# A Mamba-2 block and a quantized feed-forward block on one core: the state's product as two column tiles of 64 rows

## The chip, the cores and the metric

One core of a Trainium2 chip. The metric is the device time of one execution in microseconds (us). The engines are TensorE (PE, with its weight loads as PEld), VectorE (DVE), ScalarE (ACT), GpSimd (POOL) and SyncE (SP, which issues the transfers).

## What is computed

Two residual blocks over x of 4 x 1024 x 256 in float32: x plus the layer norm of a Mamba-2 layer, then x plus the layer norm of a feed-forward layer with 4-bit weights. The part that the change touches is the Mamba-2 layer's recurrence, cut here to its products:

```python
Y_diag = jnp.einsum('bclgn,bcsgn,bgrcls,bcsgrp->bclgrp', Cc, Bc, Lmat, xdt)
decay_states = jnp.exp(A_cs[..., -1:] - A_cs)
states = jnp.einsum('bcsgn,bgrcs,bcsgrp->bcgrpn', Bc, decay_states, xdt)
...
def step(S, inp):
    d, st = inp
    S_new = S * d[..., None, None] + st
    return (S_new, S)
...
Y_off = jnp.einsum('bclgn,bcgrpn,bgrcl->bclgrp', Cc, prev_states, state_decay)
Y = (Y_diag + Y_off).reshape(B_, nc, CHUNK, NHEADS, HEADDIM)
```

There are 8 heads of 64 channels (512 together) and 128 state rows. The kernel works in chunks of 128 positions. `states`, for one chunk, is a product of 128 state rows x 128 positions with 128 positions x 512 channels: this is "the state's product".

## The kernel before

The 4096 positions are cut into blocks of 512, each of two halves of 256, each of two chunks of 128. A loop runs 7 times over iterations (i = 2 to 8) after a first stretch of its own (`FIRST`) and before a last one (`LAST`). In one iteration the Mamba-2 part of one block is interleaved with the feed-forward part of the block before. Every engine works through a list of steps written out by hand (`ORDER`, L70; `FIRST`, L103), where `st:1` is step `st` for chunk 1 of the block, "<" marks the block before and ">" the next one. Engines synchronize by semaphores, one for each kind of step; `count` gives the value to wait for.

TensorE's steps that matter here:
- `gu:n` (L1219) and `dn:n` (L1228): the feed-forward's gate and up products (two times six matmuls with 512 columns, into the banks `fb`) and its down product (12 matmuls with 256 columns, into `db`). All go through the helper `split_matmul`, whose matmul is L1073; the operands are split in two float32r parts.
- `yo` (L1169): the state before the chunk times C, one float32 product of 128 x 128 weights and 512 columns.
- `yd` (L1177): the diagonal product. For each of 8 heads two matmuls, one for each 64 rows of the output (`l0`), with 64 columns of `lmat` as weights and 64 columns of `xdt` moving (L1184). The rows `l0` to `l0 + 63` of the bank are also the columns of TensorE's array that the matmul uses.
- `st` (L1188): the state's product, one float32 product with all 128 columns of the transposed B (`gb[:, 2 + c, :]`) as weights and the 512 columns of `xdd` moving (L1193), into one bank. It waits for GpSimd's `xdd` (L548), ScalarE's copy of B (L673) and for the reader of the product that had the bank before (`bank_read`: three banks `mb` are used in turn by all Mamba-2 steps). VectorE adds the result to the state (`state_`, L927).
- `xt`, `xtr`, `yt`, `x1t`: transposes (L1092, L1166, L1199, L1216); `ip`, `z`, `out`: projections (L1073 into `mb`).

A float32 matmul stands in the trace as two weight loads and two matmuls, a float32r one as one of each.

In the loop's order on TensorE, the four state products stand so:

```python
dn:3< yd:0 st:0 gu:6< yt:0 xtr:1 dn:4< out:0 yo:1 dn:5< yd:1 st:1 xt:1 gu:7< yt:1 ...
gu:12< dn:10< yo:2 xtr:2 xt:0> gu:13< yd:2 st:2 dn:11< yt:2 dn:12< xtr:3 out:2 yo:3 yd:3 gu:14< st:3
dn:13< yt:3 gu:15< ...
```

So `st:0`, `st:1` and `st:2` stand directly behind a diagonal product, and `st:3` between `gu:14` and `dn:13`. In `FIRST` three of six are apart from `yd` (`st:2`, and `st:1` and `st:3` of the next block). 32 state products run in all.

Of the kernel before, what the change touches and what calls it, by code (L numbers as in the profile page):

```python
# [31 lines left out]
HEADS, HD, DI, NSTATE, TAPS = 8, 64, 512, 128, 4  # L32
# [194 lines left out]
def build(nc, u, in_proj, conv_w, conv_b, dt_bias_in, a_log, d_skip, norm_w, out_proj,  # L227
          packed, scales, out):
    ctx = ExitStack()
    with ctx:  # L230
        def sb(name, shape, dt=F32, stack=ctx):
            return stack.enter_context(nc.sbuf_tensor(name, shape, dt))

        def sem(name):
            return ctx.enter_context(nc.semaphore(name))
# [81 lines left out]
        gb = sb("gb", [P, 4, CH])  # L317
        xdd = sb("xdd", [P, DI])
# [45 lines left out]
        s = {name: sem("s_" + name) for name in per_block}  # L364
        whole = ("gate", "up", "gelu", "inter", "hi", "lo", "down", "var4", "rstd4", "d_read", "fin_link")

        def count(name, i, k):

            absent = 0 if name in whole else per_block[name] // 2
            return i * per_block[name] - absent + (k + 1)  # L370
# [12 lines left out]
        m_bank = {use[:2]: mb[n % 3] for n, use in enumerate(m_uses)}  # L383
# [670 lines left out]
        def _(pe):  # L1054
            def bank_read(uses, use, i):

                u = [v[:2] for v in uses].index(use)
                it = i - AWAY[uses[u][2]]
                v, back = u, 0
                while not isinstance(it, int) or it - back >= -1:  # L1060
                    v -= 3
                    if v < 0:
                        v, back = max(w for w in range(len(uses)) if w % 3 == u % 3), back + 1
                    name, k, whose, step = uses[v]
                    if there(step, k, it - back + AWAY[whose]):
                        pe.wait_ge(s[read_by[name]], count(read_by[name], it - back + AWAY[whose], k))
                        return
# [120 lines left out]
            def st(i, par, q):  # L1188
                c = q % 2
                pe.wait_ge(s["xdd"], count("xdd", i, q))  # L1190
                pe.wait_ge(s["gbs"], count("gbs", i, q // 2))
                bank_read(m_uses, ("st", q), i)
                pe.matmul(m_bank["st", q][:], gb[:, 2 + c, :], xdd[:], start=True, stop=True).then_inc(s["st"], 1)  # L1193

            def yt_(i, par, q):
                pe.wait_ge(s["y"], count("y", i, q))
# [31 lines left out]
            def dn(f, par, n):  # L1228
# [5 lines left out]
                for t in tiles(f):  # L1234
# [5 lines left out]
                last.then_inc(s["down"], 1)  # L1240

            drive(pe, "pe", dict(xt=xt, ip=ip, cs=cs, ct=ct, seg=seg, z=z, gb=gb_, xtr=xtr, yo=yo, yd=yd, st=st, yt=yt_, out=out_,
                           x1t=x1t_, gu=gu, dn=dn), identity)

# [40 lines left out]
```

## Time and profile before

| | us |
|---|---|
| median of 3 runs | 996.51 (996.26 to 999.14) |
| the profiled execution | 1000.16 |
| its span, first to last instruction | 998.4 |
| TensorE matmuls busy | 909.1 (91%) |
| VectorE busy | 789.2 (79%) |
| ScalarE busy | 599.2 (60%) |
| GpSimd busy | 338.6 (34%) |

The first 60 us or so load and unpack weights. From then on TensorE is nearly always busy, in iterations of about 112 us each. Matmuls overlap in the pipeline: a record's duration holds its way through the array, and a group of records that follow each other takes less than their sum. The chain of waits counts each instruction from where the one before it ended, and is the better view for what a step costs in sequence. The granted clock of TensorE is 1.00 (2.4 GHz) in the steady iterations, and 0.5 in some stretches of the first 90 us.

### The profile page before, as it was taken

What the parts mean: (1) busy time and instruction counts of PE and PEld (TensorE: products, weight loads), DVE (VectorE), ACT (ScalarE), POOL (GpSimd) and SP (SyncE); (2) the same over time, 40 slices, a digit from 0 to 9 for tenths busy, and PEclk for the clock granted to TensorE, in tenths of its full rate; (3) what the DMA queues carried; (4) which work ended last, traced back from release to release, by engine and by line L of the source; (5) the groups of instructions that cost most, each with busy time, mean ns of one, the idle gap of its engine ahead of it and who ended that gap; (6) DMA issues with size and microseconds to landing.
All of it is one profiled execution on the core that took longest, in us unless ns stands there. A gap on an engine that the chain in (4) does not pass through costs nothing.

```text
span 998.4 us, 17980 instructions
## 1 busy us (share of the span) xinstructions
PE 909.1 (91%) x6560; PEld 786.0 (79%) x6560; DVE 789.2 (79%) x2079; ACT 599.2 (60%) x1013; POOL 338.6 (34%) x346
## 2 busy tenths in 40 slices
PE   1556797999999999999999999999999999999987
PEld 0445695888888788888888798878888798888887
DVE  6898777898879988898879988898879888886132
ACT  5955847574737665674737565674838565672222
POOL 2022233334252424334152424234152524234332
PEclk9767799999999999999999999999999999999999
DMA  7300000000001000000001000000000000000000
GB/s 225 124 1 11 1 12 1 12 11 2 11 2 32 1 12 1 11 23 1 12 1 33 1 11 1 11 23 1 12 1 33 2 11 2 5 18 1 1 22 11
DMA packets 14087, 17.70 MB, mean 18 GB/s; under 512 B 1712, under 2 KB 10416, under 8 KB 14000
## 3 DMA queue, kind: packets, MB, share of 16 engines
q1 hardware_dynamic: 13136, 16.53, 5.4%
q8 instruction: 52, 0.85, 0.4%
q14 instruction: 35, 0.29, 0.1%
q10 hardware_dynamic: 864, 0.03, 0.0%
HBM read 12.36 MB, written 4.19 MB: 17 GB/s over the span
## 4 chain that ended last, share of the span: by engine, by line
PE 58%; DVE 22%; ACT 7%; issue 6%; POOL 5%; DMA 1%; SPq 1%; DVEq 0%; POOLq 0%; ACTq 0%
PE fb L1073 23%; PE mb L1073 14%; PE db L1073 11%; DVE xc L882 7%; PE mb L1193 2%; DVE lmat L856 2%; DVE hid L990 2%; DVE lmat L901 2%; POOL yg L557 2%; DMA wd_raw<-in_packed 1%; PE mb L1174 1%; PE mb L1199 1%; PE mb L1184 1%; POOL hl L569 1%; ACT xc L651 1%
## 5 line engine op out<-in xcount | busy, mean ns | idle before, releaser
L569 POOL TENSOR_TENSOR hl<-hid,hl 128x512 fp32r<-128x512 f32 (+1 forms) x144 | 169.5, 1178 | 407.9 <-ACT hl L705 407.7
L1073 PE MATMUL fb<-x1t,wg 128*128 128x512 f32 (+1 forms) x864 | 215.9, 386 | 5.3 <-DVE x1t L984 5.3
L1073 PE MATMUL db<-wd,hl 128*128 128x256 f32 x1536 | 216.6, 289 | 2.2 <-POOL hl L569 2.0
L1073 PEld LDWEIGHTS db<-wd,hl 128*128 128x128 f32 x1536 | 197.4, 189 | 17.8 <-issue 10.1
L1073 PE MATMUL fb<-x1t,wu 128*128 128x512 f32 (+1 forms) x864 | 206.1, 375 | 3.3 <-ACT hid L698 3.3
L1073 PEld LDWEIGHTS fb<-x1t,wu 128*128 128x128 f32 x864 | 153.6, 192 | 36.7 <-ACT hid L698 4.8
L1073 PEld LDWEIGHTS fb<-x1t,wg 128*128 128x128 f32 x864 | 146.3, 193 | 30.9 <-DVE x1t L984 6.7
L990 DVE TENSOR_TENSOR hid<-fb,hid 128x512 f32<-128x512 f32 (+1 forms) x144 | 90.2, 627 | 78.1 <-PE fb L1073 67.6
L705 ACT ACTIVATE hl<-hid 128x512 fp32r<-128x512 f32 (+1 forms) x144 | 83.6, 581 | 106.1 <-DVE hid L990 77.8
L882 DVE SCALAR_TENSOR_TENSOR xc<-raw,cw,xc 128x256 f32<-128x256 f32 x288 | 132.9, 529 | 9.6 <-ACT xc L651 8.3
L698 ACT ACTIVATE hid<-fb 128x512 f32<-128x512 f32 (+1 forms) x144 | 78.1, 548 | 84.8 <-PE fb L1073 81.1
L1073 PE MATMUL mb<-xnt,wi 128*128 128x256 f32 x576 | 80.0, 292 | 17.9 <-DVE xnt L794 15.6
L539 POOL TENSOR_TENSOR rs<-ve,neg_half 128x1 f32<-128x1 f32 (+2 forms) x89 | 58.8, 661 | 100.2 <-DVE ve L780 30.9
L1073 PEld LDWEIGHTS mb<-xnt,wi 128*128 128x128 f32 x576 | 74.2, 197 | 19.5 <-issue 18.8
L548 POOL TENSOR_TENSOR xdd<-xdt,ex 128x512 f32<-128x512 f32 x32 | 33.4, 1043 | 116.4 <-DVE xdt L910 116.4
L698 ACT ACT_TABLE_LOAD x51 | 65.4, 1283 | 0.9
L856 DVE TENSOR_SCALAR lmat<-mb,ct_ 128x128 f32<-128x128 f32 x208 | 56.5, 342 | 2.2 <-PE mb L1130 2.2
L1073 PE MATMUL mb<-wi,xnt 128*128 128x264 f32 (+1 forms) x384 | 55.1, 295 | 3.4 <-ACT xc L651 3.4
L1073 PE MATMUL mb<-wo,yt 128*128 128x256 f32 x384 | 54.6, 293 | 3.5 <-issue 2.1
L1073 PEld LDWEIGHTS mb<-wi,xnt 128*128 128x128 f32 x384 | 51.2, 200 | 3.5 <-issue 3.5
L1073 PEld LDWEIGHTS mb<-wo,yt 128*128 128x128 f32 x384 | 49.5, 197 | 4.8 <-issue 2.9
L557 POOL TENSOR_TENSOR yg<-yg,t 128x512 f32<-128x512 f32 x32 | 42.1, 1317 | 20.4 <-DVE t L917 20.4
(150 smaller groups left out, 1360.4 us busy)
## 6 DMA issues: line engine op xcount, KB each, us to landing
xin<-in_u SPq DMA_DIRECT2D x16, 256.0 KB, 2.7
out<-xb SPq DMA_DIRECT2D x16, 256.0 KB, 2.2
wg_raw<-in_packed SPq DMA_DIRECT2D x4, 256.0 KB, 13.2
wg_raw<-in_scales SPq DMA_DIRECT2D x4, 256.0 KB
wu_raw<-in_packed SPq DMA_DIRECT2D x4, 256.0 KB, 13.6
wu_raw<-in_scales SPq DMA_DIRECT2D x4, 256.0 KB
wd_raw<-in_packed SPq DMA_DIRECT2D x4, 256.0 KB, 13.2
wd_raw<-in_scales SPq DMA_DIRECT2D x4, 256.0 KB
```

The lines of the kernel that those rows point to most:

```text
L539: pool.tensor_tensor(dst, src, neg_half[:, 0:src.shape[1]], ALU.pow).then_inc(s["rstd" + name], 1)
L548: pool.tensor_tensor(per_head(xdd[:]), per_head(xdt[:]), spread_heads(ex[:, q // 2, 1, q % 2, :]), ALU.mult).then_inc(s["xdd"], 1)
L557: pool.tensor_tensor(yg[:], yg[:], t1[:], ALU.add).then_inc(s["yskip"], 1)
L569: pool.tensor_tensor(hl[:, hs, n % 2, 1, :], hid[:, hs, n % 2, :], hl[:, hs, n % 2, 0, :].bitcast(F32), ALU.subtract).then_inc(s["lo"], 1)
L698: act.activation(hid[:, halves(f), n % 2, :], by_half(f_bank["gate", n], f), ACT.Gelu_apprx_tanh).then_inc(s["gelu"], 1)
L705: act.activation(hl[:, halves(f), n % 2, 0, :], hid[:, halves(f), n % 2, :], ACT.Copy).then_inc(s["hi"], 1)
L856: last = dve.tensor_scalar(lmat[:, c, h0 + h, :], m_bank["seg", k][:, CH * h:CH * h + CH], ct_[:, 0, r:r + 1], 0.0, ALU.subtract, ALU.min)
L882: ins = dve.scalar_tensor_tensor(out=xc[:, ct, :], in0=raw[:, slot, e, tap:tap + SUB], scalar=cw[:, ct, tap:tap + 1], in1=xc[:, ct, :], op ...
L901: dve.tensor_tensor(lmat[:, c, :, :], lmat[:, c, :, :], gb[:, c, :].unsqueeze(1).broadcast_to([P, HEADS, CH]), ALU.mult).then_inc(s["m"], 1)
L990: dve.tensor_tensor(hid[:, halves(f), n % 2, :], by_half(f_bank["up", n], f), hid[:, halves(f), n % 2, :], ALU.mult).then_inc(s["inter"], 1)
L1073: last = pe.matmul(ps, lhs(a, k), rhs(b, k), start=start and n == 0, stop=stop and n == len(todo) - 1, skip_group_check=check)
L1193: pe.matmul(m_bank["st", q][:], gb[:, 2 + c, :], xdd[:], start=True, stop=True).then_inc(s["st"], 1)
```

## The change

The state's product is done as two matmuls, each with 64 of the 128 state rows: the weights are 64 columns of the transposed B, the output is half of the bank's rows, and both have all 512 columns of `xdd` moving. The array is then addressed in halves of 64 columns, as in `yd`. The semaphore is raised behind the second.

```diff
@@ def st(i, par, q) @@
                 pe.wait_ge(s["xdd"], count("xdd", i, q))
                 pe.wait_ge(s["gbs"], count("gbs", i, q // 2))
                 bank_read(m_uses, ("st", q), i)
-                pe.matmul(m_bank["st", q][:], gb[:, 2 + c, :], xdd[:], start=True, stop=True).then_inc(s["st"], 1)
+                for n0 in range(0, NSTATE, HD):
+                    last = pe.matmul(m_bank["st", q][n0:n0 + HD, :], gb[:, 2 + c, n0:n0 + HD], xdd[:], start=True, stop=True)
+                last.then_inc(s["st"], 1)
```

`NSTATE` is 128 and `HD` 64. The orders of all engines, the waits and the other steps stay as they are.

## Rows read from the trace of the kernel before

**Rows 1.** The page, busy time: engine, us (share of the span), instructions.

```profile
PE 909.1 (91%) x6560; PEld 786.0 (79%) x6560; DVE 789.2 (79%) x2079; ACT 599.2 (60%) x1013; POOL 338.6 (34%) x346
```

**Rows 2.** Busy time by stretch, one iteration: length; PE, PEld, DVE, ACT, POOL; clock.

```profile
336.98:448.90 111.92, 110.15 (x804) 94.60 (x800) 95.04 (x256) 69.54 (x113) 40.56 (x39) 1.00 0.04 11
```

**Rows 3.** The chain in order of time, before `st:1`: start, length, what.

```profile
337.16 1.27 POOL yg L557
...
348.26 0.49 DVE xb L963
```

**Rows 4.** The chain in order of time, the state products and their neighbours.

```profile
78.76 2.04 PE mb L1193 x2
...
133.45 1.10 PE mb L1193 x2
...
348.89 1.10 PE mb L1193 x2
...
387.31 2.81 PE fb L1073 x12
390.12 1.08 PE mb L1184 x32
391.20 1.05 PE mb L1193 x2
...
399.55 3.00 PE fb L1073 x12
402.55 0.86 PE mb L1193 x2
403.41 1.43 PE db L1073 x12
...
850.50 0.86 PE mb L1193 x2
897.15 1.05 PE mb L1193 x2
908.25 1.10 PE mb L1193 x2
```

**Rows 5.** Instructions in order of time, weight loads (PEld) at `st:0`.

```profile
337.22 0.30 PEld L1193 LDWEIGHTS mb<-xdd,gb 128*128 128x128 f32 x2
```

**Rows 6.** The same for `yd:0`, in windows that end ever later.

```profile
336.13 0.14 PEld L1184 LDWEIGHTS mb<-xdt,lmat 128*64 128x64 f32 x2
336.13 0.20 PEld L1184 LDWEIGHTS mb<-xdt,lmat 128*64 128x64 f32 x4
...
336.13 0.34 PE L1184 MATMUL mb<-xdt,lmat 128*64 128x64 f32 x4
336.13 1.15 PE L1184 MATMUL mb<-xdt,lmat 128*64 128x64 f32 x32
```

**Rows 7.** Lines 1184 and 1193: count, duration min/median/max in ns.

```profile
L1184 PEld LDWEIGHTS mb<-xdt,lmat x1024: 132/138/194, 60.1 to 907.8; 128*64 128x64 f32 x171
L1184 PE MATMUL mb<-xdt,lmat x1024: 221/222/333, 60.1 to 907.9; 128*64 128x64 f32 x171
...
L1193 PEld LDWEIGHTS mb<-xdd,gb x64: 186/188/339, 58.6 to 908.3; 128*128 128x128 f32 x64
L1193 PE MATMUL mb<-xdd,gb x64: 590/592/1190, 58.6 to 908.8; 128*128 128x512 f32 x64
```

**Rows 8.** Instructions in order of time, PE, around `st:1`.

```profile
347.68 0.57 PE L1184 MATMUL mb<-xdt,lmat 128*64 128x64 f32 x13
348.89 1.10 PE L1193 MATMUL mb<-xdd,gb 128*128 128x512 f32 x2 [0.63 <-DVE xb L963]
349.82 0.60 PE L1092 MATMUL mb<-ident,xn 128*128 128x128 f32 x4
```

**Rows 9.** Instructions in order of time, weight loads at `st:3`.

```profile
402.16 0.42 PEld L1193 LDWEIGHTS mb<-xdd,gb 128*128 128x128 f32 x2
```

**Rows 10.** The chain in order of time, around the first state product.

```profile
58.56 2.04 POOL state L554
```

## The prediction

> **What bounds the kernel now.** I read four things. The page's first lines and the split by iteration say which engine is full: TensorE is busy 909.1 of 998.4 us, and from the third iteration on it is busy 110.1 of each 112.0 us at the full granted clock (2.4 GHz), with the idle rest in a few short waits [rows 1, 2]. VectorE, at 95 of 112, is the second. A shorter or longer TensorE instruction therefore moves the end only where the chain of waits runs through TensorE, so I read that chain in order of time next. It is split in two in every iteration: a part that alternates between VectorE, ScalarE and GpSimd (from the convolution to the first chunk's layer norm), and a part that is TensorE alone, from the second chunk's state product (`st:1`) on, through `st:2` and `st:3` [rows 3, 4]. `st:0` lies in the first part and is not on the chain, but for the last iteration. Of 32 state products 22 are on it: 8 that start after a wait, with 1.10 us each (7 `st:1` and one more of the same kind at 133.45), 7 isolated ones with 0.86 us (`st:3`), 6 directly behind the diagonal product with 1.05 us, and one at 78.76 in the slow-clock start with 2.04 us [rows 3, 4].
>
> **What the array mode costs today.** The diagonal product `yd` has 64 columns of weights, everything around it 128. The chain shows what going in and out costs. Out: twelve `fb` matmuls take 2.81 us behind ordinary work and 3.00 us behind `yd`; a state product takes 0.86 us behind ordinary work and 1.05 us behind `yd` [rows 4]. Both give about 0.20 us. The weight-load rows say what it is made of. The 32 records of `yd` end at 337.28, and one lasts 0.22, so the last started at 337.06; the load of `st:0` starts 0.16 us later, at 337.22, with nothing streaming behind it, where in ordinary work a load runs under the matmul before it [rows 5 to 7]. In: the 32 instructions of `yd` take 1.08 us on the chain; inside it four end at 0.34 and 32 at 1.15 us, so 0.81/28 = 0.029 us each, 0.93 us for 32, which leaves 0.15 us for going in [rows 4, 6].
>
> **What the two column tiles cost.** Each float32 product is two instructions (64 records for 32 products) of 0.43 us (0.86/2), or 0.84 ns a column [rows 4, 7]. After the change there are four, each still streaming all 512 columns of `xdd`, since splitting the state rows splits the weights and not the moving side. So the product gains nothing by itself; the question is whether the tiles run side by side. `yd` is the nearest row, with the same pattern of two instructions on one half, then two on the other. At 0.84 ns a column one of its 64-column instructions needs 0.054 us, and 32 of them in turn would need 1.72 us; they take 0.93. Their weight loads show how: the first two fill 0.14 us together, where one alone takes 0.138 (so they started together), and four fill 0.20 [rows 6, 7]. Two loads of full width, those of `st:0`, fill 0.30 us where one takes 0.19, so they start one after the other [rows 5, 7]. So in `yd` the two halves run at once, and I take 2 x 0.43 + 0.01 = 0.87 us for the four. The bounds: 0.43 us (if a half streamed at twice the rate) and 4 x 0.43 = 1.72 us (no overlap). I choose 0.87 because the same pattern stands in the trace, only with shorter streams.
>
> The Trainium skill (TensorE: Matmul & The Clock Gate, "Measured speedup vs the span model") would give one duration plus some 4 ns per further tile, which is the same 0.87. Its neighbour section "The mechanism", with "What overlaps and what doesn't", says that matmuls keep program order and only weight loads are pulled ahead. By that rule the other half's first instruction could not start before this half's second, which is rival 1 below and would make the time 1010.4. The trace so far is against it.
>
> **The change part by part, on the chain.**
> (a) `st` directly behind `yd` with no wait (`st:0`, `st:2`; 6 on the chain). Before: out of the mode (0.20), then 0.86. After: 0.87, then out of the mode in front of the next group. The 0.20 moves from ahead of `st` to behind it; net 0.01 each, 0.06 us in all. Queued behind it are the next `gu` or `dn`; the only reader of the product is VectorE's add (L927), which stands in its order behind the diagonal's add and the 1024-wide `decayed_products:1`, so that the result comes 0.2 us earlier buys nothing.
> (b) `st` behind a wait (`st:1`; 8 on the chain). VectorE's read of the bank (L963) releases it [rows 3, 8]: the last records of `yd` end at 348.25 and the product starts at 348.89, so today the array empties under the wait and only the weight load shows. After: the load is of 64 columns instead of 128, 138 against 188 ns [rows 7], a gain of 0.05; the way out, 0.20, now comes behind `st` with nothing to cover it, since the transposes `xt:1` behind it are ready and start without a gap [rows 8]. Net +0.15 + 0.01, 8 x 0.16 = 1.3 us. If the way out were covered, it would be -0.05.
> (c) `st` alone among full-width work (`st:3`, behind `gu:14`, before `dn:13`; 7 on the chain). There are two switches more: in 0.15 and out 0.20, plus 0.01: 7 x 0.36 = 2.5 us. No wait stands around it: the load of `st:3` starts at 402.16, 0.23 us before its first matmul, under `gu:14`, and `dn` follows at once [rows 4, 9], so nothing hides either switch. Bounds per piece: 0 (all hidden) and 0.50 (both with a full load and a drain behind a 512-column stream).
> (d) The one at 78.76 runs at half clock, its own instructions take twice as long; it waited too, so as (b), 0.2 us. The product at 58.6 is not on the chain, which runs through GpSimd's work there [rows 10]: I put it at nothing; uncovered it is 0.2.
> Sum: 0.06 + 1.3 + 2.5 + 0.2 = 4.0 us. Nothing else moves: no step, wait or queue of another engine is touched. Since each of these pieces is on a chain that is TensorE work back to back, the delay goes through; late next is whatever TensorE issues, and VectorE's part begins that much later.
>
> The profiled execution took 1000.16 us with a span of 998.4; I expect 1004.2 for it. The median of the runs shown is 996.51, so 3.7 lower; with the same 4.0 it becomes 1000.5 us (+0.40%).
>
> **The rivals.**
> 1. The halves start in program order only: `xdd` has to start its second pass through the first half before the other half may begin. Then three streams of 0.43 us instead of two, +0.43 for 21 products on the chain and +0.86 at the half clock: 9.9 us more, 996.51 + 4.0 + 9.9 = 1010.4. For it: long streams in halves stand nowhere in this trace, and 32 short ones in such a stagger would need 17 slots of 0.054, 0.92 us, so the length of `yd` can't exclude it. Against it: the weight loads that start in pairs [rows 6]: in a stagger the first of them would stand alone.
> 2. No overlap at all: +0.86 each, 1.7 at the half clock: 19.8 more, 1020.3. `yd` at 0.93 instead of 1.72 speaks against it.
> 3. The other side: a half streams faster than the full array does. `yd`'s pace of 0.058 us a pair could be set by its weight loads, so that its streams don't show. If four 512-column instructions then took 0.43 us in all, each product would win 0.43: -9.9 + 4.0, 990.6, faster. It decides once the product takes less than 0.68 us (22 x 0.19 = 4.2). Against it: matmul medians are 222 ns with 64 columns in halves and 592 with 512 in full width, 370/448 = 0.83 ns a column across the two modes, as within one [rows 7].
> 4. The switches are partly hidden in the isolated places (c), or the later ones are taken up in VectorE's part: with half of (c) and (b) some 2 us remain, 998.5.
>
> **How the numbers follow.** Forecast 1000.5 with 0.76 (its own range 999.0 to 1002.5, from (b) and (c) between 0.6 and 1.5 of their price); rival 4 0.11; rival 1 0.07; rival 2 0.02; rival 3 0.04. From 997.5 to 1003.0 holds the forecast and most of rival 4, together about 0.85; the edges are outcomes of the bounds in (c). What this kernel's measurement can tell from no change is about 0.3%, 3.0 us, so the forecast lies just above it: slower takes 0.68 of the forecast's 0.76 and both of rivals 1 and 2, 0.77; within 0.3% takes the other 0.08 and rival 4 less a little, 0.18; faster 0.05.
>
> **What would show it.** In the changed kernel's trace: 128 matmul records of the state product, 128x512 in 128*64, in a group that lasts about 0.87 us per product from the first stream to the last; the chain's row of the group behind an `st` longer by 0.20 (`dn` 1.63 instead of 1.43), with no 0.16 us step between the last matmul of `yd` and the load of `st:0`; iterations of 112.5 instead of 112.0 us. A product at 1.3 us means rival 1, at 0.43 rival 3. An unchanged iteration with rows as described would mean that TensorE's delay is taken up, which would make (b) and (c) wrong though the switch prices are right.

## The result

| | before | changed |
|---|---|---|
| median of 14 runs, us | 996.16 (994.92 to 1000.89) | 1000.17 (998.28 to 1002.29) |
| ratio to before | | 1.0033, 95% interval 1.0023 to 1.0043 |
| profiled execution, us | 1000.16 | 999.05 |
| its span, us | 998.4 | 997.3 |
| one steady iteration, `yd:2` to `yd:2`, us | 111.94 | 112.43 |

The change makes the kernel slower by 3.3 us by the ratio (2.3 to 4.3), 4.0 by the medians. The profiled execution of the changed kernel is nevertheless 1.1 us shorter in its span. That is its start: it reaches the first `yd:2` of the loop 3.8 us sooner than the profiled execution of before. The start differs from one execution to the next whatever the product's form (last section). From there to the end it is longer, 997.3 - 274.2 = 723.1 against 998.4 - 278.0 = 720.4. The weight loads of `yd:2` in three iterations that follow each other (start, length, what; [idle before]), before first:

```profile
278.02 1.01 PEld L1184 LDWEIGHTS mb<-xdt,lmat 128*64 128x64 f32 x32 [0.36 <-issue]
...
390.05 1.01 PEld L1184 LDWEIGHTS mb<-xdt,lmat 128*64 128x64 f32 x32 [0.36 <-issue]
...
501.99 1.01 PEld L1184 LDWEIGHTS mb<-xdt,lmat 128*64 128x64 f32 x32 [0.36 <-issue]
```

and in the changed kernel:

```profile
274.23 1.01 PEld L1184 LDWEIGHTS mb<-xdt,lmat 128*64 128x64 f32 x32 [0.36 <-issue]
...
386.76 1.01 PEld L1184 LDWEIGHTS mb<-xdt,lmat 128*64 128x64 f32 x32 [0.36 <-issue]
...
499.19 1.01 PEld L1184 LDWEIGHTS mb<-xdt,lmat 128*64 128x64 f32 x32 [0.36 <-issue]
```

The last two of each give the iteration: 501.99 - 390.05 = 111.94 us before, 499.19 - 386.76 = 112.43 changed. The other steady iterations lie within 0.1 us of these, but for one that is about 0.25 longer in either kernel, while whole runs of one kernel lie up to 6 us apart. So the experiments below are read by this length, always of the same iteration and from the same rows of their traces, by the mean of the five iterations from the first `yd:2` of the loop to the last, and by the ratio. One iteration and the mean of five agree within 0.05 us on what a version adds, so a hundredth of a microsecond of one iteration says nothing.

Busy time of the changed kernel on its page (columns as in [rows 1]), then the product in the groups by shape, before (L1193) and changed (L1194); a group gives busy us and mean ns of one, then idle time before and its releasers:

```profile
PE 911.2 (91%) x6624; PEld 777.3 (78%) x6624; DVE 791.6 (79%) x2079; ACT 598.9 (60%) x1013; POOL 338.7 (34%) x346
```

```profile
L1193 PE MATMUL mb<-xdd,gb 128*128 128x512 f32 x64 | 35.9, 644 | 9.7 <-DVE xb L963 7.7 <-POOL xdd L548 2.0
...
L1194 PE MATMUL mb<-xdd,gb 128*64 128x512 f32 x128 | 34.1, 607 | 9.0 <-DVE xb L963 7.0 <-POOL xdd L548 2.0
```

There are 64 matmul records more (128 instead of 64 for the product), of about the old length (607 ns on average, 644 before), and their group is busy for 34.1 us, where the 64 were for 35.9: twice the instructions in no more time.

The chain of the changed kernel in order of time around the three state products of an iteration that are on it (start, length, what), which answers to [rows 4]:

```profile
345.45 1.08 PE mb L1194 x4
346.53 0.59 PE mb L1092 x4
347.12 2.81 PE fb L1073 x12
...
386.83 1.08 PE mb L1184 x32
387.92 0.86 PE mb L1194 x4
388.78 1.63 PE db L1073 x12
390.40 0.65 PE mb L1201 x4
...
396.27 3.01 PE fb L1073 x12
399.27 1.01 PE mb L1194 x4
400.28 1.63 PE db L1073 x12
401.91 0.44 PE mb L1201 x4
```

Three rows of the same view of the kernel before that [rows 4] don't have: the transposes `xt:1` behind `st:1`, `xtr:2` behind `yo:2`, and `yt:2`:

```profile
349.98 0.44 PE mb L1092 x4
...
386.44 0.44 PE mb L1166 x4
...
393.69 0.64 PE mb L1199 x4
```

`st:2` (387.92) is 0.86 instead of 1.05 and the `dn` behind it 1.63 instead of 1.43: the way out has moved. `st:3` (399.27) is 1.01 instead of 0.86 and `dn:13` 1.63 instead of 1.43: a way in and a way out were added. `st:1` (345.45) is 1.08 instead of 1.10, and the transposes behind it 0.59 instead of 0.44.

The weight loads of `st:2` in the changed kernel show the two halves:

```profile
387.69 0.20 PEld L1194 LDWEIGHTS mb<-xdd,gb 128*64 128x64 f32 x4
388.70 0.54 PEld L1073 LDWEIGHTS db<-wd,hl 128*128 128x128 f32 x4 [0.81 <-issue]
```

Four loads fill 0.20 us, as in `yd` [rows 6], and they start before those of `yd` have ended (386.76 + 1.01): the 0.16 us ahead of the load of `st:0` before have no counterpart here, as the prediction's sign asked. Then the first load of `dn` comes 1.01 us behind them, after 0.81 us without any load, when the product's two streams of 0.43 us are through.

### The profile page after: what moved, and what is told of

The parts are those of the page before. It is cut to its first block, busy times and chain, and to the rows that moved or that the text cites. A ratio compares the mean times of both kernels' runs of the same rounds, so it can differ in the third digit from the quotient of the medians.

```text
span 997.3 us, 18108 instructions
## 1 busy us (share of the span) xinstructions
PE 911.2 (91%) x6624; PEld 777.3 (78%) x6624; DVE 791.6 (79%) x2079; ACT 598.9 (60%) x1013; POOL 338.7 (34%) x346
## 4 chain that ended last, share of the span: by engine, by line
PE 58%; DVE 21%; ACT 8%; issue 6%; POOL 5%; DMA 1%; SPq 1%; DVEq 0%; POOLq 0%; ACTq 0%
PE fb L1073 22%; PE mb L1073 13%; PE db L1073 12%; DVE xc L882 6%; PE mb L1194 2%; DVE lmat L856 2%; DVE hid L990 2%; DVE lmat L901 2%; POOL yg L557 2%; PE mb L1174 2%; DMA wd_raw<-in_packed 1%; PE mb L1201 1%; PE mb L1184 1%; POOL hl L569 1%; ACT xc L651 1%
## 5 line engine op out<-in xcount | busy, mean ns | idle before, releaser
L1073 PE MATMUL fb<-x1t,wg 128*128 128x512 f32 (+1 forms) x864 | 213.0, 382 | 5.9 <-DVE x1t L984 5.1
L1073 PE MATMUL db<-wd,hl 128*128 128x256 f32 x1536 | 213.5, 287 | 2.2 <-POOL hl L569 2.1
L683 ACT ACTIVATE yt<-mb 128x512 fp32r<-128x512 f32 x32 | 19.1, 597 | 51.0 <-PE mb L1201 51.0
```

What stands on the lines that cost most here:

```text
L1073: last = pe.matmul(ps, lhs(a, k), rhs(b, k), start=start and n == 0, stop=stop and n == len(todo) - 1, skip_group_check=check)
```

## The experiments

Two theories stand against each other. One: a product in halves costs nothing in itself, and what costs is each way in and out of the array mode (products that use TensorE's array in column tiles of 64) that nothing covers. The other: every halved product costs something wherever it stands. Each run is told by the length of one steady iteration (the same one, `yd:2` to `yd:2`) and by its ratio to the kernel before.

| run | iteration, us | mean of five, us | ratio (95% interval) |
|---|---|---|---|
| before | 111.94 | 111.99 | |
| changed | 112.43 | 112.49 | 1.0033 (1.0023 to 1.0043) |
| e1: isolated products whole | 112.06 | 112.16 | 1.0010 (0.9997 to 1.0022) |
| e2: isolated products alone halved | 112.30 | 112.36 | 1.0030 (1.0018 to 1.0043) |
| e3: changed, `st:3` joined to `yd:3` | 112.09 | 112.17 | 1.0022 (1.0010 to 1.0034) |
| e3b: before, the same move | 111.93 | 112.02 | 1.0006 (0.9997 to 1.0015) |
| e4: `yo` halved | 112.02 | 112.09 | 1.0012 (1.0000 to 1.0023) |
| e5: four quarters | 112.42 | 112.50 | 1.0038 (1.0021 to 1.0055) |
| e6: one half only | 112.37 | 112.46 | 1.0024 (1.0012 to 1.0037) |
| e7: `yd` whole | 113.05 | 113.10 | 1.0091 (1.0078 to 1.0104) |
| e8: `gu:7` ahead of `st:1` | 113.10 | 113.19 | 1.0073 (1.0061 to 1.0085) |
| e9: only `yo:2` halved | 112.05 | 112.09 | one execution, no ratio |

### e1 and e2: where the cost lies

```diff
-                for n0 in range(0, NSTATE, HD):
-                    last = pe.matmul(m_bank["st", q][n0:n0 + HD, :], gb[:, 2 + c, n0:n0 + HD], ...)
+                rows = NSTATE if q == 3 and i > 0 or (i, q) in ((0, 2), (1, 1)) else HD
+                for n0 in range(0, NSTATE, rows):
+                    last = pe.matmul(m_bank["st", q][n0:n0 + rows, :], gb[:, 2 + c, n0:n0 + rows], ...)
```

e2 has `HD` and `NSTATE` exchanged in that line.

> The changed kernel, with the isolated state products (st:3 of every block but the first, and the two of the start) whole again as in the kernel before, all others in halves. Theory (what the change costs is the way in and out of the array mode where nothing covers it): st:3 loses its 0.15 + 0.20 + 0.01, so an iteration from one yd:2 to the next is 0.36 shorter than the changed kernel's 112.43 us: 112.07, against 111.94 before; the whole kernel 4.0 - 2.7 = 1.3 us slower than before. Rival (the products in halves are what costs, wherever they stand: more instructions, more loads): a quarter of the cost goes, 112.31.

> The complement: only the isolated state products in halves, those behind yd whole. Theory: an iteration of 111.94 + 0.36 = 112.30 us, the whole 2.7 us slower than before. Rival (every halved product costs alike): 111.94 + 0.12 = 112.06, 1.0 us slower.

e1 measured 112.06 where 112.07 was expected, e2 112.30 where 112.30 was. The quarter of the products that stands alone carries 0.36 or 0.37 of the 0.49 us, the other three quarters 0.12 or 0.13, and the two parts add up to the whole. By the means of five iterations it is 0.33 to 0.36 of 0.50 against 0.13 to 0.17. That the cost goes with the product and not with its place is refuted. The ratios go the same way: 1.0 and 3.0 us against 1.3 and 2.7 expected, within their intervals.

### e3 and e3b: the same halves, joined to `yd`

```diff
-        ... yo:3 yd:3 gu:14< st:3
+        ... yo:3 gu:14< yd:3 st:3
```

> The changed kernel with gu:14 ahead of yd:3 instead of between yd:3 and st:3, in the loop's order on TensorE: then st:3 stands directly behind yd:3 and shares its array mode. Theory: the two added switches go, 0.35 us less, an iteration of 112.08 us, and only 0.14 more than its own control without halves. yd:3 comes 2.8 us later, and yt:3 stands 4.9 us behind its old end, so there should be no new wait; if there is one, it shows in the control too.

> The control: the kernel before with the same move of gu:14. The way in and out of the mode is paid once round yd:3 as ever, so nothing changes: 111.94 us an iteration, within 0.5 us of the kernel before. If VectorE, which gets yd:3 2.8 us later, becomes late for yt:3 or the next block, the iteration grows in both.

The isolated product became a neighbour of `yd:3` and lost its own way in and out: 112.09 us with halves, 111.93 without. The chain of e3 in order of time:

```profile
397.28 2.80 PE fb L1073 x12
400.08 1.08 PE mb L1184 x32
401.16 0.86 PE mb L1194 x4
402.02 1.63 PE db L1073 x12
```

So 0.34 us come back by a move in the order alone, with all products in halves, and the move itself costs nothing in the control (-0.01). What is left over the control is 0.16, most of it the way out behind `st:1` (0.13, below). The edit changes the loop's order only, so six of the seven isolated products on the chain are joined: 4.0 - 6 x 0.35 = 1.9 us, a ratio of 1.0019 by the theory, and 1.0022 was measured.

### e6: do the halves stream side by side

```diff
-                for n0 in range(0, NSTATE, HD):
+                for n0 in (0,):
```

> The changed kernel with only the first half of the state's product: the output rows 64 to 127 are left out (the bank's old values are read), so its output is not the reference's. If the two halves stream side by side, the second costs nothing: a product keeps 0.86 on the chain and the iteration 112.43 us less 0.01 for each of three products, the whole stays within 0.5 us of the changed kernel. If they ran in a stagger, the product would fall from 1.3 to 0.86, if one after the other from 1.72 to 0.86.

This kernel leaves out half of the state's rows, and the iteration is 0.06 us shorter (0.03 in the mean of five). Its chain:

```profile
387.25 0.85 PE mb L1194 x2
388.10 1.63 PE db L1073 x12
...
398.60 1.00 PE mb L1194 x2
```

Two instructions take 0.85 us where four took 0.86: the second half is free to 0.01 us. Behind the wait of `st:1` it saves a little more, 1.04 instead of 1.08 on the chain. A stagger or a sequence is out. One half alone also pays the ways in and out (1.00 + 1.63 at `st:3`), so they go with the mode and not with the number of instructions.

### e5: four quarters

```diff
-                for n0 in range(0, NSTATE, HD):
-                    last = pe.matmul(m_bank["st", q][n0:n0 + HD, :], gb[:, 2 + c, n0:n0 + HD], ...)
+                rows = 32
+                for n0 in range(0, NSTATE, rows):
+                    last = pe.matmul(m_bank["st", q][n0:n0 + rows, :], gb[:, 2 + c, n0:n0 + rows], ...)
```

> The changed kernel with the state's product in four column tiles of 32 rows (eight instructions). Theory: the four tiles stream side by side, 0.87 us a product as with two; and if going from 64 to 32 columns is a change of mode like the others, st:2 pays it (about 0.10 to empty the array and 0.03 for a load of 32 columns) on top of the way out: 112.43 + 0.13 - 0.05 for the shorter loads = 112.5 us. If all column modes were one, 112.4. If at most two tiles stream at once, 0.86 more for each product: three on the chain, 115.0.

The iteration is 112.42, not 112.5, which alone would read as: from 64 to 32 columns there is no switch. The chain says otherwise:

```profile
387.73 0.99 PE mb L1195 x8
388.73 1.63 PE db L1073 x12
390.35 0.55 PE mb L1202 x4
...
399.11 0.99 PE mb L1195 x8
```

`st:2` behind `yd` has grown from 0.86 to 0.99, by the 0.13 expected, and `st:3` has shrunk from 1.01 to 0.99, with eight instructions, four at a time. But the transposes `yt:2` are 0.55 where the changed kernel has 0.65: 0.10 us of the delay disappears there. So the price was right and its way to the end was not; e4 and e9 show why. That a change of mode lies between 64 and 32 columns rests on this row of the chain alone, since the iteration's length is the one that the theory without it gave.

### e4 and e9: another product in halves

e4 halves `yo` everywhere, e9 only `yo:2`, in the kernel before:

```diff
-                pe.matmul(m_bank["yo", q][:], xc[:, 5, CH * c:CH * c + CH], state[:], ...)
+                rows = HD if q == 2 else CH
+                for l0 in range(0, CH, rows):
+                    last = pe.matmul(m_bank["yo", q][l0:l0 + rows, :], xc[:, 5, CH * c + l0:CH * c + l0 + rows], state[:], ...)
```

> The kernel before, with another product in halves: yo, the state times C, as two column tiles of 64 positions. yo:2 stands alone on the part of the chain that is TensorE's; yo:3 stands directly ahead of yd:3, so that the way in only moves; yo:0 and yo:1 stand alone in VectorE's part, ahead of the wait of 0.63 us at st:1. Theory: yo:2 costs 0.36 (0.15 in, 0.20 out, 0.01), yo:3 0.01, yo:0 and yo:1 0.72 together, of which the wait takes 0.63: 0.36 to 0.46 in all, an iteration of 112.30 to 112.41, the whole 2.6 to 3.4 us slower. Rival (every halved product costs alike, 0.12 to 0.17): 112.4 to 112.6 with yo:2 and yo:3 costing the same; the rows of the chain tell the two apart.

This missed: 112.02 instead of 112.30 to 112.41. The chain of e4:

```profile
382.83 1.01 PE mb L1175 x4
383.84 0.59 PE mb L1166 x4
...
391.25 0.44 PE mb L1201 x4
...
394.96 1.01 PE mb L1175 x4
395.96 0.93 PE mb L1186 x32
```

`yo:3` (394.96) is 0.15 longer and `yd:3` behind it 0.15 shorter: the way in moved, at no cost, as expected. `yo:2` (382.83) pays 0.15 for the way in, and the transposes `xtr:2` behind it 0.59 instead of 0.44, so that the way out costs 0.15 there and not 0.20. That is 0.30 in sum, but 0.20 of it is given back at `yt:2`: 0.44 instead of 0.64. What is left, 0.10, is the iteration's growth (0.08, or 0.10 in the mean of five). In the kernel before, `yt:2` (393.69) waits. The instructions in order of time there:

```profile
393.67 0.42 PEld L1199 LDWEIGHTS mb<-ident,yg 128*128 128x128 f32 x4 [0.18 <-DVE yg L935]
```

I had read TensorE's part of the chain as back to back because a piece of PE followed each piece of PE; the wait of 0.18 us for VectorE's `yg` is inside the length of one of them. A delay that comes shortly ahead of `yd:2` is taken up there, until 0.2 us are spent. And what `yo:0` and `yo:1` add in VectorE's part comes out of the wait at `st:1`, which falls from 0.63 [rows 8] to 0.06:

```profile
344.98 1.08 PE mb L1186 x32
346.06 0.06 issue
346.12 1.10 PE mb L1195 x2
```

> The kernel before with only yo:2 of each block in halves. In the run with all yo in halves the chain's rows grew by 0.30 around yo:2 (0.15 in, 0.15 out ahead of the transposes) but the iteration only by 0.10, and the row of yt:2 fell from 0.64 to 0.44. Theory: TensorE has a wait of 0.20 us for VectorE hidden in that row, which takes up any delay that comes right before yd:2; then this run gives 112.04 us and a yt:2 of 0.44. Rival (yo:0 or yo:1 made the 0.10, and yo:2 costs nothing for another reason): 111.94, yt:2 still 0.64; or, with no such slack, 112.24.

e9 measured 112.05 with `yt:2` at 0.44, as its theory had it, in one execution:

```profile
385.38 1.01 PE mb L1176 x4
386.39 0.59 PE mb L1166 x4
...
393.80 0.44 PE mb L1202 x4
```

So `yo:2` alone makes the 0.10, and the slack at `yt:2` is real.

### e7: no array mode at all

```diff
-                    for l0 in range(0, CH, HD):
-                        last = pe.matmul(m_bank["yd", q][l0:l0 + HD, HD * h:HD * h + HD], lmat[:, c, h, l0:l0 + HD], ...)
+                    last = pe.matmul(m_bank["yd", q][:, HD * h:HD * h + HD], lmat[:, c, h, :], ...)
```

> The kernel before without the array mode anywhere: the diagonal product with 128 columns of weights, 16 instructions of 64 columns a chunk instead of 32. Theory: no way in (0.15) and out (0.20) any more, but each instruction needs a full load, 128 columns; at the 0.107 us between the starts of two such loads that is 16 x 0.107 = 1.71 us instead of 0.93. Net 0.78 - 0.35 = +0.43 for yd:2 and yd:3 each: 112.8 us an iteration, 6 to 7 us slower in all. If the streams set the pace (0.054 each), 0.86 us and 0.42 less each: 111.1.

```profile
390.36 1.73 PE mb L1183 x16
392.09 0.91 PE mb L1192 x2
...
399.02 1.73 PE mb L1183 x16
400.75 2.85 PE fb L1073 x12
```

16 instructions take 1.73 us, 0.108 each, twice the 0.054 of a 64-column stream: the full weight loads set the pace, as expected. Against 1.08 + 1.05 before, 1.73 + 0.91 is 0.51 more at `yd:2` and 1.73 + 2.85 against 1.08 + 3.00 is 0.50 more at `yd:3`, where 0.43 was expected (the instruction behind is 0.05 late, for which I had no term). The iteration grew by 1.11, not by 0.86: 0.81 of it is these two less the 0.20 taken up at `yt:2`; the other 0.3 must come from `yd:0` and `yd:1`, whose 1.0 us is more than the 0.63 of the wait at `st:1` could take: on the chain of e7 that wait is gone, and `st:1` follows `yd:1` directly. I had left that part at zero, and the whole kernel is some 9 us slower by the ratio, not 6 to 7. For `yd` the array mode earns its ways in and out.

### e8: an attempt at a faster order

```diff
-        ... yd:1 st:1 xt:1 gu:7< yt:1 ...
+        ... yd:1 gu:7< st:1 xt:1 yt:1 ...
```

> The kernel before (all whole), with gu:7 between yd:1 and st:1 instead of behind xt:1, in the loop's order on TensorE. TensorE waits 0.63 us ahead of st:1 for VectorE's read of the bank; gu:7 needs nothing of that and would fill it. Theory: the part behind it is TensorE alone, so an iteration gets up to 0.63 shorter than 111.94: 111.3 us, the whole some 4 us faster. Rival: st:1 and xt:1 come 2.2 us later, ScalarE and VectorE take xt:1 ahead of their parts of gu:7 in their orders and stand still until then, and yt:1 and the bank fb wait for them: no gain, or slower by what they lose, up to 2 us an iteration.

The rival came true: 113.10 us. As it said, VectorE stands still for what `xt:1` brings: it waits 1.26 us for ScalarE's copy (L602) and reads the bank of `st:1` (L927) only behind that. What waits on TensorE is neither `yt:1` nor the bank `fb`, as the rival had it, but `ip:3`, which needs the bank of `st:1` (instructions in order of time):

```profile
349.54 1.02 PE L1193 MATMUL mb<-xdd,gb 128*128 128x512 f32 x2
350.40 0.60 PE L1092 MATMUL mb<-ident,xn 128*128 128x128 f32 x4
350.83 0.60 PE L1199 MATMUL mb<-ident,yg 128*128 128x128 f32 x4
353.10 1.66 PE L1073 MATMUL mb<-xnt,wi 128*128 128x256 f32 x12 [1.67 <-DVE state L927]
```

0.63 us filled, 1.67 us opened. None of the versions tried beats the kernel before.

## Why the prediction was right, and where it was off

The forecast was 1000.5 us; the median is 1000.17, and the ratio's 3.3 us (2.3 to 4.3) holds the 4.0 of the sum. That the medians differ by just 4.0 is partly luck, as the interval of the ratio is 2 us wide; the iteration is the sharper test, 0.49 us more where the parts give 0.53 (0.01 + 0.16 + 0.36). The forecast for the profiled execution, 1004.2 us, missed: it took 999.05, for the start that differs from execution to execution and that the prediction had taken as fixed. By its steps:

- The bound and its two parts. TensorE's part carries the cost, as said: `st:1` to `st:3` with their 0.49 us an iteration. That it is back to back was too strong: it has a wait of 0.18 us at `yt:2`. In this change it mattered nothing, since the delays of this change don't arise right ahead of it: `yt:2` is 0.65 on the chain of the changed kernel, as it was 0.64 before.
- The product in halves at 0.87 us. It is 0.86, with loads in pairs as read from `yd`. e6 shows that the second half is free. Rivals 1, 2 and 3 fall with it. The Trainium skill (TensorE: Matmul & The Clock Gate, "What overlaps and what doesn't") has matmuls start in program order. If both passes of one half stand ahead of the other half's first, as the order of the source suggests, the product would take 1.3 us by that rule, and the trace is against it; but the trace doesn't name the half that a record belongs to, so the order of the four in the program is not shown. The span model of the Trainium skill ("Measured speedup vs the span model"), one duration and a few ns, agrees with the 0.01 us of e6.
- (a) Behind `yd` without a wait. 0.86 + 1.63 against 1.05 + 1.43: 0.01 us, as said.
- (b) Behind a wait. Net 1.08 + 0.59 against 1.10 + 0.44: 0.13 instead of 0.16. Two sizes were off and nearly cancel. The way out costs 0.15 and not 0.20 ahead of transposes; e4 shows the same 0.59 at `xtr:2`. And the shorter load gains 0.02 and not 0.05: one half alone takes 1.04 (e6), which is 0.06 less than the whole product, but the second half adds 0.04, as after a wait it starts later than in a running stream. In the windows of the changed kernel at `st:1`, the four loads fill 0.23 us instead of 0.20:

```profile
345.42 0.23 PEld L1194 LDWEIGHTS mb<-xdd,gb 128*64 128x64 f32 x4 [0.62 <-POOL xdd L548]
```

- (c) Isolated. 0.15 in, 0.20 out: 1.01 + 1.63 against 0.86 + 1.43 is 0.35, and e1, e2 and e3 show 0.37, 0.36 and 0.34 in the one iteration, 0.33, 0.36 and 0.32 in the mean of five. The largest term was right, and neither switch is hidden.
- (d) The product at the start. In the changed kernel's profiled execution it stands at full clock, 1.08 us instead of 2.04, which is the execution's start and not the change. The execution of e3 has it in halves at the half clock: 1.98 us with 1.06 for the transposes behind it, where the kernel before has 2.04 and 0.87. That is 0.13 instead of 0.2.
- The sum with the measured sizes is 0.06 + 8 x 0.13 + 7 x 0.36 + 0.13 = 3.75 us, against 4.0 predicted. The steady part can be checked in the traces, from the first `yd:2` of the loop to the `yd:0` of the last block (895.99 us before, 895.04 changed): five iterations of 0.49 and the `st:2` and `st:3` behind them, 0.37, make 2.8, and 620.81 - 617.97 = 2.84 was measured. Behind it 0.14 more were due for the last `st:0` and `st:1`, but the stretch to the end is 0.15 shorter (102.26 against 102.41), so that 2.7 are left in all. In the twelve traces but e7's this stretch is between 102.1 and 102.9 us long, whatever the product's form, so it can't show 0.14.
- Rival 4, with part of the cost taken up, did not come true here, but its mechanism exists: it took 0.20 us from e4 and 0.10 from e5. It takes up what comes shortly ahead of `yt:2`, at `yo:2` or `st:2`, but not what `st:1` or `st:3` add: those delay VectorE as well. That last reason is argued from the rows and not measured by itself.

## What to carry to other kernels

With 512 moving columns, two column tiles don't make a product with full-width weights faster, since both halves stream all columns; they stream side by side, so they don't make it slower either. With 64 moving columns they do make it faster (e7), because there the full-width load sets the pace and not the stream. What is paid is the change of the array mode: 0.15 us in and 0.15 to 0.20 out on a busy TensorE, so put steps of one mode next to each other, and count switches, not instructions. Before trusting that a stretch of the chain is TensorE back to back, compare the length of each piece with others of its kind: one that is 0.2 us too long hides a wait, and a delay just ahead of it can cost that much less.

## What the runs showed of the hardware

Going from one column mode to another (64 to 32 columns) costs 0.13 us on the chain (`st:2` in e5, 0.99 instead of 0.86), much as going in from full width does (0.15, `st:3` in the changed kernel). The way out is 0.20 us ahead of `gu` or `dn` (2.81 to 3.00 and 1.43 to 1.63) and 0.15 ahead of float32 transposes (0.44 to 0.59).

The start of this kernel differs from one execution to the next by more than the change is worth. The windows of 78 to 95 us, before first, then changed (length; PE, PEld, DVE, ACT, POOL; clock):

```profile
78.00:95.00 17.00, 13.66 (x74) 11.74 (x75) 13.64 (x40) 8.86 (x16) 3.87 (x3) 0.71 0.05 17
```

```profile
78.00:95.00 17.00, 11.96 (x92) 10.89 (x91) 15.87 (x48) 12.97 (x23) 3.87 (x3) 1.00 0.05 17
```

One had TensorE's clock at 0.71 on average there, the other at 1.00 (2.4 GHz). Together with a first weight transfer of 14.63 against 13.64 us on the chain, this goes with the 3.8 us by which the changed kernel's profiled execution was ahead at 274 us. How much of it is the clock wasn't measured, and it isn't the clock of this stretch alone: e3b has 0.78 there. Nor is it the change: the first `yd:2` of the loop comes at 274.4 us in e3b, with whole products, and at 277.4 in e2, with the isolated ones in halves; over the twelve traces it lies between 273.6 and 278.1. Half clock is not over at 90 us either: from 95 to 115 us the mean is 0.75 before and 0.74 changed. A comparison of two spans would have called the change a gain of 1.1 us.
